# The first value product of a head group moved one step earlier, with a wait of its own for each piece

## What is computed

```python
x = layernorm(x + attention(x))      # x: (16, 512, 128) f32, 16 heads of 8, causal
x = layernorm(x + experts(x))        # layernorm, top-2 gate of 8 experts, 128 -> 512 -> 128, gelu
# attention, for every batch element and head:
Q, K, V = heads(x @ Wq), heads(x @ Wk), heads(x @ Wv)
scores = where(causal, -1e6, Q @ K.T / sqrt(8))     # 512 x 512
attn = softmax(scores) @ V                          # then @ Wo + bo
```

## Time and profile before

| | |
|---|---|
| median of 3 runs | 984.21 us (983.76 to 986.77) |
| profiled execution, its own time | 991.02 us |
| its span, first to last instruction | 989.3 us |
| granted clock of TensorE, mean | 0.967 |
| PE busy with matmuls | 854.8 us, 86% |
| DVE busy | 743.5 us, 75% |
| ACT busy | 677.1 us, 68% |
| POOL busy | 657.1 us, 66% |

### The profile page before, as it was taken

One profiled execution on the slowest core, in us unless ns is written; L12 is line 12 of the kernel. 1 busy time (PEld: TensorE's weight loads), 2 busy tenths in 40 slices (PEclk: granted clock), 3 DMA queues, 4 the chain that ended last, 5 costly groups with the idle time before them and its releaser, 6 DMA issues.

```text
span 989.3 us, 28895 instructions
## 1 busy us (share of the span) xinstructions
PE 854.8 (86%) x9151; PEld 564.2 (57%) x9151; DVE 743.5 (75%) x2021; ACT 677.1 (68%) x1433; POOL 657.1 (66%) x906
## 2 busy tenths in 40 slices
PE   4688898888989989989999988779999999999960
PEld 2334354444444444444444444349999989989950
DVE  1787778888988898889889889845554555377767
ACT  1277687777777777877877877746566555667863
POOL 6243555778777777787787786766767656567652
PEclk9799999999999999999999999979999999999985
DMA  7624635536446355355354342253233323276544
GB/s 197 196 69 158 176 93 163 161 106 206 127 146 211 97 171 174 96 166 158 93 185 129 112 153 73 61 143 83 79 85 88 85 72 96 78 248 181 170 128 139
DMA packets 168771, 132.37 MB, mean 134 GB/s; under 512 B 52845, under 2 KB 154516, under 8 KB 168496
## 3 DMA queue, kind: packets, MB, share of 16 engines
q1 hardware_dynamic: 156336, 112.34, 38.4%
q0 software_dynamic: 8640, 17.06, 5.1%
q10 hardware_dynamic: 3648, 1.12, 0.5%
HBM read 71.42 MB, written 61.01 MB: 134 GB/s over the span
## 4 chain that ended last, share of the span: by engine, by line
PE 39%; POOL 8%; issue 5%; ACT 5%; DVE 3%; DMA 2%; DVEq 0%; ACTq 0%; POOLq 0%; SPq 0%
PE ring L1241 14%; PE ring L1257 13%; PE ps_v L1177 3%; POOL probs L672 2%; PE ring L1114 2%; ACT probs L804 2%; POOL rs L738 1%; POOL rows_d L714 1%; PE ps_v L1231 1%; PE ring L1145 1%; DVE probs L1643 1%; PE ps_m L991 1%; DVE negmax L1301 1%; POOL qarea L636 1%; PE ps_m L1013 1%
## 5 line engine op out<-in xcount | busy, mean ns | idle before, releaser
L1301 DVE TENSOR_REDUCE negmax<-ring 128x2 f32<-128x1024 f32 (+3 forms) x512 | 407.5, 813 | 67.9 <-PE ring L1160 66.6
L804 ACT ACTIVATE probs<-ring 128x768 f32<-128x768 f32 (+1 forms) x384 | 334.8, 879 | 116.6 <-PE ring L1114 111.9
L672 POOL TENSOR_SCALAR_AFFINE_SELECT probs<-probs 128x512 f32<-128x512 f32 x256 | 162.4, 637 | 160.2 <-ACT probs L804 158.1
L928 ACT ACTIVATE vpad<-ring,b_s 128x128 f32<-128x128 f32 x568 | 162.2, 368 | 106.3 <-PE ring L1241 104.1
L722 POOL DMA_INDIRECT y_d<-vpad,xs x142 | 149.1, 1050 | 89.1 <-DVE vpad L1612 60.0
L1177 PE MATMUL ps_v<-probs,vpad 128*32 128x512 f32 (+3 forms) x2048 | 183.4, 448 | 10.4 <-POOL probs L672 10.4
L1257 PE MATMUL ring<-qarea,vpad 128*128 x1136 | 153.9, 279 | 3.4 <-issue 3.0
L1241 PE MATMUL ring<-vpad,w_t 128*128 128x128 f32 x1136 | 154.3, 280 | 2.8 <-issue 1.3
L714 POOL DMA_INDIRECT rows_d<-xn,slot x128 | 128.9, 1007 | 30.1 <-issue 27.1
L1241 PEld LDWEIGHTS ring<-vpad,w_t 128*128 128x128 f32 x1136 | 139.7, 194 | 5.7 <-issue 3.2
L1257 PEld LDWEIGHTS ring<-qarea,vpad 128*128 128x128 f32 x1136 | 137.8, 192 | 8.5 <-issue 7.0
(11 more groups left out here) (195 smaller groups left out, 1177.2 us busy)
## 6 DMA issues: line engine op xcount, KB each, us to landing
kside<-qk_d SPq DMA_DIRECT2D x32, 512.0 KB, 5.3
qk_d<-qarea SPq DMA_DIRECT2D x32, 384.0 KB, 2.7
xs<-rows_d SPq DMA_DIRECT2D x142, 66.0 KB, 1.9
qk_d<-qarea SPq DMA_DIRECT2D x32, 256.0 KB, 2.4
qarea<-qk_d SPq DMA_DIRECT2D x16, 512.0 KB
qodd<-qk_d SPq DMA_DIRECT2D x16, 512.0 KB
probs<-y_d SPq DMA_DIRECT2D x16, 512.0 KB, 5.1
xin<-L_attn_x SPq DMA_DIRECT2D x16, 256.0 KB, 3.9
```

What stands on the lines that cost most here:

```text
L672: pool.affine_select(out=diag, in_=diag, pattern=[[0, 4], [1, P]], compare_op=ALU.is_ge, fill=0.0, base=0, channel_multiplier=-1).then_inc ...
L804: nc.scalar.activation(of_unit(h // 2, part), ring[:, 2 * part % 3, :, (0, P, P)[part]:S], ACT.Exp, scale=SCALE).then_inc(sem("exp_done"), 1)
L928: ins = nc.scalar.activation(ht[:, n % 4, c, :], ps_a[:, n % 4, c * P:(c + 1) * P], ACT.Gelu_apprx_tanh, bias=b1_s[:, bass.ds(e, 1), c:c + ...
L1301: ins = nc.vector.tensor_reduce(negmax[:, n // 6 % 2, qb, s:s + 2], ring[:, (2 * n + 1) % 3, :, c0:c0 + nk], AX.X, ALU.max, negate=True)
```

## The change

v0 goes from the end of a group's second step to the end of its first, behind m1 and ahead of s2. v1 and v2 stay. The wait for masks, of which v0 had one for all four masks of its group, is now in each piece: v0 and v1 wait for the third (an even step's, the last that touches blocks 0 and 1), v2 for the fourth.

```diff
@@ def values(b, g, kbs):
                 if not b.exists(NB):
                     return
+                need(pe, sem("masked"), NH, b, GH * (g + 1) - (kbs[-1] < 2))
                 if kbs[0] == 0:
-                    need(pe, sem("masked"), NH, b, GH * (g + 1))
                     if g == 0:
                         need(pe, freed("v"), 1, b, 1)
@@ def body(i):
-                    if h % 4:
+                    if h % 4 != 1:
                         vb, vg = (i, h // 4 - 1) if h >= 4 else (i.plus(-1), 3)
-                        values(vb, vg, ((0,), (1,), (3, 2))[h % 4 - 1])
+                        values(vb, vg, ((0,), None, (1,), (3, 2))[h % 4])
```

## The result

The changed kernel takes 991.01 us (median of 20 runs, 987.58 to 994.83), the kernel before, on the same chip, 987.67 us (median of 20, 981.04 to 994.23). The ratio is 1.0038, with a 95% interval of 1.002 to 1.0055: slower, by 2.0 to 5.4 us. The forecast was slower by 8.3.

The account below looks back on a forecast made before the run. It took a chain from DVE's second maximum and s1 of step 14 through mask, roots and ACT to m1 of step 2 as the bound. Terms 7.6 + 0.7 gave +8.3 us on 984.2: 992.5 us, range 983.5 to 996.5.

Parts of the forecast that it names:

- the main term: Steps 12 to 14 of 13 iterations: v0 delays m2, DVE's maxima and s1 by 0.59 us each, +7.6 us in all.
- the chain of steps 0 to 2: From the roots through ACT's normalisation and exponentials to m1 of step 2; v0's removed 0.67 us wait gives 0, within 0.1.
- Steps 12 to 14: DVE's first maximum of m2 comes 0.59 us later, and s1 of step 14 with it, in each iteration.
- Steps 4 to 6: The later exponential of s2 stays hidden behind ACT's copies of V and a normalisation, with 0.17 us to spare: 0.
- Steps 8 to 10: The exponential of s2 comes 0.10 us later in nine iterations, 0.05 gained in four: +0.7 us, between 0 and 1.3.
- PE's waits for DVE: In the profile after the change, PE's waits for DVE were to grow by some 5 to 7 us.
- The sum, 13 x 0.59 = +7.6 us: The 0.59 us delay of steps 12 to 14 charged in all 13 iterations 2 to 14, less 0.1: +7.6 us.
- The third rival: Slower, but less: the clock stays up, both falls in the iterations' thin stretches go, 989.1 us; chance 0.15.
- The first rival: Faster: v0's 8.1 us of waits for masks in step 1 are real and saved, 975 us; chance 0.09.
- The carry-over: The whole kernel's forecast +8.3 us, added to a median of 984.2 us, 6.8 under the profiled execution: 992.5 us.

Follow-up runs that it names:

- Experiment 9: The changed kernel with ACT's normalisations of step 1 moved to step 3; 1045.49 us, ratio 1.002 to the kernel before.
- experiment 1: The changed kernel with v0 put back in step 13 in the last group only; 985.31 us, ratio 0.9988 to the kernel before.
- experiment 2: The changed kernel with v0 moved in the last group only, the other three groups' v0 left in the second step; 988.27 us, ratio 1.0017 to the kernel before.
- experiment 4: The changed kernel with DVE's four statistics placed behind the second maximum of m2; 989.36 us, ratio 1.0039 to the kernel before.
- experiment 3: The kernel before with the changed kernel's separate waits, every v0 left where it was; 983.02 us, ratio 0.9967 to the kernel before.
- light transfers: Second expert matrix read directly, first loaded in iterations 8 to 15; kernel before 1037.27 and 1031.66 us, changed kernel 1045.81 and 1045.43 us.
- experiment 10: The kernel before with ACT's normalisations of step 1 moved to step 3; 1043.26 us, ratio 1.0 to the kernel before.
- experiment 7: The kernel before with lighter expert-weight transfers in iterations 0 to 7, run again on another chip; 1031.66 us, ratio 0.9915 to the kernel before.
- experiment 8: The changed kernel with lighter expert-weight transfers in iterations 0 to 7, run again on another chip; 1045.43 us, ratio 1.0029 to the kernel before.

## Why the prediction was right, and where it was too high

The direction was right (slower), and 991.01 us lies in the range. The mechanism of the main term was right too; what was wrong is how often it falls due.

- *v0 isn't on the chain of steps 0 to 2.* Right. Its wait is gone, and m1 of step 2 came 7.97 us after the mask of step 14, where it was 8.04; 0 was forecast, within 0.1. Experiment 9 shows the chain itself: with ACT's part behind the roots moved away, 0.85 us go.
- *Steps 12 to 14, +0.59 us for each iteration.* Right in mechanism and place (experiments 1, 2, 4), and 0.64 in size. The 0.05 is v0's length. I took 0.95 us from the row at 534.20 in the earlier trace rows, which has only five of its eight products; the first three start at 534.10. Behind m1, with nothing interleaved, v0 takes 534.55 - 533.55 = 1.00.
- *Steps 4 to 6, 0.* Right: 4.64 us in both kernels.
- *Steps 8 to 10, +0.1 for each iteration.* 0.16 (experiment 2). It adds to the 0.64, steps 0 to 2 give back 0.05, and the settled iteration pays 0.74.
- *PE's waits for DVE, +5 to 7 us.* Wrong in sign: 5.2 us less. Only the new wait at s1 was thought of, not the waits of s2 that v0 now fills. The time doesn't hang on it.
- *The sum, 13 x 0.59 = +7.6 us: this is the term that was mis-sized.* Its premise was that "the pattern holds in the 13 iterations 2 to 14". It holds as a pattern of instructions, not as a bound. In iterations 1 to 9 the nine together cost -0.1 us with the clock falls taken out, and nothing between experiments 2 and 3. The delay arises there too, but a DMA of the turned maxima often ends last behind it and takes it up, so that only the late ones pay: 150.20 us for iterations 10 to 13 before (607.87 - 457.67, the second figure being m1 of iteration 10 and the first that of 14), and 153.00 after (609.26 - 456.26), +2.8. That lies inside what the times say (2.0 to 5.4). The first rows that I read already spoke of it: the early iterations took 38.2 to 39.7 us where the late ones took 37.74, and I took the late ones for all. With light transfers, the early ones pay +6.1 and +7.2, and the whole comes to 8.5 and 13.8 us.
- *The third rival, the clock stays up.* It came true in addition: no fall in steps 0 to 2 of any iteration of the changed kernel. Each fall cost 1.4 us in steps 0 to 2, where 1.7 was worked out. The four profiles of kernels in which v0 waits in step 1 (before, the light pair's two runs of its form, experiment 10) have 2, 2, 2 and 5 falls there, and the ten profiles in which it doesn't have none. Experiment 3 removes the same wait without moving anything and has none either, so it is the wait and not the place of v0 that matters. The rule of the Trainium skill (TensorE: Matmul & The Clock Gate, Why this matters for your kernels), to avoid idle gaps between bursts of matmuls, points the same way, but it speaks of longer gaps than the 0.67 us here; that so short a wait matters is what these traces show.
- *The first rival* (the waits of v0 are worth their 8.1 us) is refuted by experiment 3: 0.1 us each and the falls.
- *The carry-over.* 984.21 us was the median of three runs; twenty gave 987.67. The predicted time, 992.5, is near 991.01 partly because a sum that was 5.0 us too high (8.3 against 991.01 - 987.67 = 3.3) met a start that was 3.5 too low.

The change has thus a good half, the separate waits (ratio 0.9967 alone), and a bad one, the move ahead of s2 and m2 in the last group.

## What to carry to other kernels

A delay measured in a settled iteration isn't to be multiplied by the number of iterations before their lengths have been compared: where some are longer, another bound may have the last word there and take up the delay. A block moved ahead of work that another engine reduces in its own fixed order costs that engine's idle time, even when the mover's own engine has room. And a wait and a place are two changes; tested apart, one was worth keeping.

## What the runs showed of the hardware that was not expected

The same kernel takes 985.82 us on one chip and 1042.94 on another. Most of it is in the experts' phase: in the changed kernel PE starts its first product with an expert tile at 655.33 us on the first chip and at 662.25 us on that of experiments 7 and 8, where the time is also slower (1047.89 us), and the end comes 332 and 384 us later. The granted clock of TensorE is alike (0.973 and 0.963 on average), and what is slower there was not looked into.

A single wait of 0.67 us of PE, behind one of 0.62 at m1 and one of 0.27 at s2, goes with a granted clock at 1.2 in place of 2.4 GHz for about 3.4 us from the moment at which v0 starts (428.53 in iteration 10). The window there, with PEclk as the seventh figure:

```profile
428.50:431.90 3.40, 3.37 (x18) 1.07 (x19) 1.36 (x5) 2.31 (x4) 3.04 (x4) 0.50 1.05 361
```

It comes in some iterations and not in others with the same gaps (2 of the 14 iterations 2 to 15 before, 5 in experiment 10), and in these steps in no kernel without that wait.

A DMA of 16 KB whose packets are done within 1.8 us of its issue in a late iteration of the changed kernel (issued at 546.23) lands 4.20 us after it in iteration 3 of experiment 1 (157.86).
